# Results and residuals of a leftward scan moved by two DMA-issuing engines instead of one

## What is computed

```python
def step(w, b):
    def f(carry, inp):
        nxt = inp + _conv1d(carry, w, b)     # kernel width 5, 48 -> 48 channels
        return (nxt, nxt)
    return f
# down over the rows, up over them, right over the columns (R), and last:
l0 = R[Ww - 1]
_, l_rest = jax.lax.scan(step(left_w, left_b), l0, R[Ww - 2::-1])
L = jnp.concatenate([l0[None], l_rest], 0)[::-1]
...
x = x + _L1_conv_ref(_gn(x), ...)
x = x + _L2_conv_ref(_gn(x), ...)
```

## Time and profile before

| | us |
|---|---|
| median of 3 runs | 11995.99 |
| lowest, highest | 11984.39, 11999.71 |
| the profiled execution | 12018.95, of which its span 12017.2 |
| way left of layer 1 in the trace | about 5243 to 5942 |
| way left of layer 2 in the trace | about 7752 to 8680 |

### The profile page before, as it was taken

One profiled execution on the slowest core, in us unless ns is written; L12 is line 12 of the kernel. 1 busy time (PEld: TensorE's weight loads), 2 busy tenths in 40 slices (PEclk: granted clock), 3 DMA queues, 4 the chain that ended last, 5 costly groups with the idle time before them and its releaser, 6 DMA issues. The chain is left out here.

```text
span 12017.2 us, 240297 instructions
## 1 busy us (share of the span) xinstructions
PE 11090.9 (92%) x82492; PEld 10261.1 (85%) x82492; DVE 7593.3 (63%) x19405; ACT 3302.7 (27%) x3654; POOL 5471.2 (46%) x5025
## 2 busy tenths in 40 slices
PE   0999999899989998999899989999879999999999
PEld 0999999666669998998799989988779999999974
DVE  5444444322248886878788868765567776776754
ACT  0222222232222352024322540065522222222210
POOL 0666666333335554555455545544334343443410
PEclk9999999899999999999899999987689999999999
DMA  9666666699976467779865667799745555555569
GB/s 173 137 136 135 138 135 137 128 195 192 193 155 178 137 178 166 172 163 217 171 163 135 181 161 176 163 211 212 170 96 117 102 114 112 105 118 103 117 194 364
DMA packets 1973947, 1906.93 MB, mean 159 GB/s; under 512 B 1224122, under 2 KB 1863968, under 8 KB 1900960
## 3 DMA queue, kind: packets, MB, share of 16 engines
q1 hardware_dynamic: 1973152, 1897.01, 70.1%
HBM read 781.57 MB, written 578.81 MB: 113 GB/s over the span
## 5 line engine op out<-in xcount | busy, mean ns | idle before, releaser
L741 POOL TENSOR_TENSOR rl_wide<-rl_wide,rl_state 96x512 f32<-96x512 f32 x510 | 816.9, 1602 | 810.0 <-ACT rl_state L655 810.0
L273 PE MATMUL du_sum<-du_high,sw_down_high 96*96 96x256 f32 x6132 | 1081.7, 285 | 61.4 <-DVE du_high L335 33.7
L273 PE MATMUL du_sum<-du_low,sw_down_high 96*96 96x256 f32 x6132 | 1115.3, 290 | 0.1
L273 PE MATMUL du_sum<-du_high,sw_down_low 96*96 96x256 f32 x6132 | 1074.7, 283 | 0.0
L937 POOL TENSOR_TENSOR gf_own_low<-gf_sums,gf_own_high 96x2080 fp32r<-96x2080 f32 x128 | 598.4, 4675 | 903.0 <-DVE gf_hid_a L1517 898.0
L1433 PE MATMUL gf_four<-gf_own_high,l_w_hid_high 96*128 96x256 f32 x3072 | 884.1, 288 | 109.4 <-DMA gf_next_low<-gf_own_low 109.4
L931 POOL TENSOR_TENSOR gf_sums<-gf_block 96x520 f32<-96x520 f32 x512 | 602.8, 1206 | 667.0 <-DVE gf_hid_a L1517 629.4
L937 POOL TENSOR_TENSOR qk_own_low<-qk_sums,qk_own_high 96x2080 fp32r<-96x2080 f32 x128 | 597.0, 4664 | 667.0 <-ACT qk_own_high L901 667.0
L273 PEld LDWEIGHTS du_sum<-du_high,sw_down_high 96*96 96x96 f32 x6132 | 828.1, 164 | 69.1 <-DVE du_high L335 35.5
L1433 PE MATMUL gf_four<-gf_next_high,l_w_hid_low 96*128 96x256 f32 x3072 | 874.4, 285 | 0.0
L1433 PE MATMUL gf_four<-gf_own_low,l_w_hid_high 96*128 96x256 f32 x3072 | 873.3, 284 | 0.0
(11 more groups left out here) (214 smaller groups left out, 32283.9 us busy)
## 6 DMA issues: line engine op xcount, KB each, us to landing
qk_next_high<-qk_own_high SPq DMA_DIRECT2D x256, 389.8 KB, 5.2
qk_next_low<-qk_own_low SPq DMA_DIRECT2D x256, 389.8 KB, 5.3
gf_next_high<-gf_own_high SPq DMA_DIRECT2D x256, 389.8 KB, 5.4
gf_next_low<-gf_own_low SPq DMA_DIRECT2D x256, 389.8 KB, 5.5
du_wide<-x SPq DMA_DIRECT2D x32, 3072.0 KB, 17.0
up<-du_wide SPq DMA_DIRECT2D x32, 3072.0 KB, 20.9
rl_wide<-up SPq DMA_DIRECT2D x128, 768.0 KB, 15.8
rl_wide<-x SPq DMA_DIRECT2D x128, 768.0 KB, 16.6
```

Of the source, the lines that this page charges most:

```text
L273: mm = self.nc.tensor.matmul(self.half_line(r, c), w[0:kk, k, :], x[0:kk, (r - 1) % RING, 2 * c:2 * c + 2, k:k + PAIRS], start=(n == 0 and ...
L741: nc.gpsimd.tensor_tensor(at, at, by_sub_block(row), ALU.add).then_inc(placed, 1)
```

## The change

On the way left ScalarE takes over, on its own DMA queue, the two pieces of each store and of each residual load that lie on partitions 48 to 95. SyncE keeps the other two. Blocks 0 to 2 are still loaded whole by SyncE, and block 15 is stored whole by it. ScalarE issues the store of block m - 1 at step r = 3 of block m, after `keep_state`, and the load for block m + 1 at step r = 5, with waits equal to SyncE's and, in layer 2, one for its own repacking of block m - 2.

```diff
+BY_BOTH = 3
+STORE_AT = 3
+LOAD_AT = 5
             def load_residual(m):
-                for d, s in pieces(residual, NB - 1 - m, results[m % 3]):
+                for d, s in pieces(residual, NB - 1 - m, results[m % 3])[0:4 if m < BY_BOTH else 2]:
                     sp.dma_start(s, d).then_inc(whole[m % 3], 16)
...
             def store_back(m):
                 sp.wait_ge(placed, BLK * m + BLK)
-                for d, s in pieces(dst, NB - 1 - m, results[m % 3]):
+                for d, s in pieces(dst, NB - 1 - m, results[m % 3])[0:4 if m == NB - 1 else 2]:
                     sp.dma_start(d, s).then_inc(back_out[m % 3], 16)
...
+            def store_half(m):
+                act.wait_ge(placed, BLK * m + BLK)
+                for d, s in pieces(dst, NB - 1 - m, results[m % 3])[2:4]:
+                    act.dma_start(d, s).then_inc(back_out[m % 3], 16)
+
+            def load_residual_half(m):
+                act.wait_ge(measured, m - 2)
+                act.wait_ge(back_out[m % 3], 64 * (m // 3))
+                if patches is not None:
+                    act.wait_ge(px_made, PX_PARTS * (m - 2))
+                for d, s in pieces(residual, NB - 1 - m, results[m % 3])[2:4]:
+                    act.dma_start(s, d).then_inc(whole[m % 3], 16)
...
                 keep_state(t)
+                m, r = (t - TURN) // BLK, (t - TURN) % BLK
+                if r == STORE_AT and m >= 1:
+                    store_half(m - 1)
+                if r == LOAD_AT and BY_BOTH <= m + 1 < NB:
+                    load_residual_half(m + 1)
```

## The result

The changed kernel is slower: 12143.31 us (median of 6 runs) against 11996.33, a ratio of 1.014, 95% interval 1.011 to 1.0169. The forecast was 11975, its range 11885 to 12075.

The account below looks back on a forecast made before the run. The prediction took layer 1 as bound by TensorE, layer 2 by the DMA engines or by TensorE at half clock. Layer 1 at 0 and layer 2 at -21 us took 11996 to 11975, range 11885 to 12075.

Parts of the forecast that it names:

- The load pair's price: ScalarE's two residual loads at step 5: at most about 2.5 us, inside the cover, so 0 in both layers.
- the far end of my own bounds: Highest issue time on ScalarE for one pair: 10.1 us with the queue full, against 0.89 us with it free.
- the far end of the sum: Worst case for layer 1: 28 pairs x (10.1 - 3.7) = 179 us lost; the forecast took 0.
- the near end: Lowest issue time on ScalarE for one pair, queue free: 0.89 us, hidden in both layers.
- The cover: How long a pair may hold ScalarE in layer 1 before TensorE waits for the fill: 3.7 us.
- Rival C: ScalarE's issues block when the path to the DMA engines is full: 106 us lost in layer 1, total 12100, chance 0.25.
- Moves, waits and landings: ScalarE's added waits are met before they are asked, and later stores and residual loads stay hidden: 0 us.
- Layer 2: Shorter waits for patches leave about one and a half fewer half-clock blocks: 21 us gained, bounds 58 gained to 18 lost.
- The sum of 57.8 us: One layer-2 block's lines, stores, residual and patches at separate rates, against 57.3 measured: DMA engines have hardly a microsecond to give.
- Rival B: Two queues overlap slow loads and fast stores in layer 2: 88 to 127 us gained, total 11870 to 11910, chance 0.18.
- D: Rival: DMA work is what counts, waits and three slow layer-2 blocks stay, total within 20 us of 11996, chance 0.20.

## Why the prediction was wrong, step by step

**The load pair's price: the step that failed.** I wrote "at step 5 it holds at most the two store pieces, and four pieces fit with 3.34 us, so the load pair costs at most about 2.5 us". It costs 10.17. The 3.34 us of the earlier trace rows are four pieces onto idle DMA engines, which begin to empty the queue at once. At step 5 of that block (5396.01) the lines have landed (5390.25), but SyncE's second store, its two loads and ScalarE's two stores are all still on their way, and ScalarE's first store, issued 5.5 us earlier, landed only 16.0 us after its issue; the pair came free 0.3 us before that landing. So it is in the other blocks: nine of the eleven long pairs came free within 0.6 us of the landing of ScalarE's first store, two 2 us behind it. What I needed was how long a piece stays in a queue when the engines are full, and the earlier trace rows showed that it is several pieces' time: the far end of my own bounds, 10.1 us from a full queue, is what the longest pairs took (the thirteen average 8.0). That the far end of the sum, 179 us for layer 1, meets the measured 180.0 is luck: it stood for 28 pairs of 6.4 us of waiting and no loss of clock, and there were 56.0 us of waiting, at eleven pairs, and 124.0 of clock. I chose the near end by how many pieces were in ScalarE's queue and not by what stood before them in the engines.

**The cover: right.** 3.7 us a pair, worked out from one late fill and the idle time, against 4.06 measured twice in layer 1. Store pairs of 3.4 us were free, as the sum needs.

**Rival C: the right mechanism at too low a price and chance.** Point, place and order were right (the pair's hold over 3.7 us, layer 1, TensorE waiting for the fill). Its 106 us took half-full pairs and 2 us of lower clock each. Layer 1 lost 180.0, of which 56.0 are waits and 124.0 the clock: 124.0/11 = 11.3 us of clock for each pair that made TensorE wait, where I had added 2. The earlier trace rows held that price: the slow blocks of layer 2 cost 13.2 us each over a normal one, and TensorE's waits there were only 51.0 us in all. I used it for the gain in layer 2 and not for the loss in layer 1.

**Moves, waits and landings: right.** The added waits cost nothing (the store pair starts at 5390.47, right behind `keep_state` at 5390.45), the later residual was in time, layer 1's steps in variants without a long hold take 696.2 us to the tenth.

**Layer 2: the right sign, a wrong reason.** Expected -21 us; the change as made gives about -10 by the runs (layer 2 alone), the kernels with later or single pieces by both engines about -35 to -43, all pieces one by one -79 and -84. ScalarE's issues, which I had put at 0 in this layer too, eat a part of it. The changed kernel's waits for patches fall from 115.7 to 84.6 us, but now there is also

```profile
ACT rl_px L670 <- issue: 63.6, 22, 7.1
```

The sentence "the DMA engines have hardly a microsecond to give in such a block" is refuted by the sixteen steps in 44.6 us with nearly the same bytes. The sum of 57.8 us came from rates of stretches in which one kind of traffic ran alone, and its agreement with 57.3 was taken for a bound. The rate depends on what runs beside what: 218 GB/s in the earlier trace rows, 277 in that stretch. A share of 1.00 said that the engines were occupied, not that they could do no more.

**Rival B: not borne out.** One queue with the same times gives the same total, and the share of the engines is 0.87 to 0.99 in kernels with two queues. **D** fell with layer 1.

Open is why spreading the pieces raises the rate of the DMA engines on one queue. The runs show that it does; none separates the order from the distances in time.

## What to carry to other kernels

A DMA issue on a compute engine is nearly free (0.33 us) if the one before it lies long enough back, here two steps or 5.5 us, and may hold the engine for 10 us if it comes right behind others on a full way; so put single issues steps apart, and price a pair by how long the piece before it stays in the queue when the engines are full. Before moving issues to another engine, try their times on the engine that has them: here that gave all of the gain (0.76%) without a second queue, while the second queue itself gave none that the runs can tell. And where a short wait of TensorE lowers its clock, price the wait with what follows: here 124 us came on top of 56.

## What was not expected of the hardware

- A first DMA of ScalarE was taken in 0.33 us while SyncE's own issue was blocked; only ScalarE's second waited (3.1 us), until 1.0 us after SyncE's ended. In a block in which SyncE issued nothing it waited as long (3.0 us).
- With 768 KB pieces the fourth piece in ScalarE's queue held ScalarE for 9.8 us and let it go 0.3 us before the first landed, though each piece two steps behind the last is handed over in 0.33 us.
- The share of busy DMA engines at the same 215 GB/s was 0.98 or 0.99 on one queue and anything from 0.87 to 0.99 on two.
- A share of 1.00 went with 218 GB/s in one block of layer 2, one of 1.07 with 277 in another.
- A wait of 6.11 us of TensorE was followed by 8.7 us at the granted clock of 0.50 (three matmuls in 0.84 us instead of 0.53), and another block ran at it for over 70 us; over the way left the clock cost 2.2 times the waits.
